# Cross attention: dividing by the softmax's sums in feature layout, after a trip through DRAM

## The reference

```python
q = split_heads(layernorm(x) @ wq + bq)        # 8 x 16 x 512 x 16
k = split_heads(ctx @ wk + bk)                 # 8 x 16 x 64 x 16
v = split_heads(ctx @ wv + bv)
scores = q @ k.T / sqrt(16) (+ mask)           # the mask in the second layer only
attn = softmax(scores, axis=-1)
x = x + (attn @ v).reshape(8, 512, 256) @ wo + bo
```

## Time and profile before

| | |
|---|---|
| time, median of 3 runs | 2571.32 us (2565.01 to 2572.29) |
| the profiled execution's own time | 2568.06 us |
| its span, first to last instruction | 2566.3 us |
| mean granted TensorE clock | 0.962 of full |
| DMA, mean over the span | 58 GB/s |

### The profile page before, as it was taken

How to read it: one execution, slowest core, us unless ns; L and a number is a source line. 1 busy time by engine, 2 the same in 40 slices (tenths; PEclk the granted TensorE clock), 3 DMA queues, 4 the chain that set the end, 5 groups by cost and what they waited for, 6 DMA issues and landing times. The chain is left out here.

```text
span 2566.3 us, 45589 instructions
## 1 busy us (share of the span) xinstructions
PE 2330.6 (91%) x14571; PEld 1519.5 (59%) x14585; DVE 1457.3 (57%) x3885; ACT 1140.1 (44%) x2685; POOL 734.6 (29%) x848
## 2 busy tenths in 40 slices
PE   7999999889996799899999999888886799999998
PEld 5455555545555566533443333445556599999997
DVE  4766676446765443577777767354545733444333
ACT  1666656523331562277777776422221033333332
POOL 3111111044421321333333221153311433333333
PEclk9999999999998999999999999999995899999999
DMA  6222222120000310322222121100009122222221
GB/s 156 88 87 90 87 76 88 31 76 5 5 1 1 105 44 1 93 63 72 66 76 68 58 73 53 40 7 9 9 1 362 57 36 33 36 36 36 36 35 22
DMA packets 135325, 148.85 MB, mean 58 GB/s; under 512 B 25286, under 2 KB 119152, under 8 KB 135024
## 3 DMA queue, kind: packets, MB, share of 16 engines
q1 hardware_dynamic: 119504, 127.23, 16.1%
q0 software_dynamic: 13680, 17.84, 4.3%
q10 hardware_dynamic: 1968, 1.60, 0.4%
HBM read 100.71 MB, written 46.01 MB: 57 GB/s over the span
## 5 line engine op out<-in xcount | busy, mean ns | idle before, releaser
L452 ACT ACTIVATE self_probs<-self_score_ps 128x512 f32<-128x512 f32 (+3 forms) x1024 | 481.0, 516 | 315.0 <-PE self_score_ps L813 162.7
L618 DVE TENSOR_REDUCE self_neg_max<-self_max_ps 128x1 f32<-128x512 f32 x512 | 328.2, 685 | 147.8 <-PE self_max_ps L799 143.3
L799 PE MATMUL self_max_ps<-self_k_stack,self_q_stack 96*128 96x512 bf16 (+3 forms) x1024 | 347.6, 342 | 21.1 <-DVE self_neg_max L615 12.3
L810 PE MATMUL self_score_ps<-self_q_stack,self_k_stack 99*128 99x512 bf16 (+3 forms) x1024 | 342.5, 342 | 1.6 <-ACT self_probs L452 1.6
L2259 ACT ACTIVATE x_stream<-experts_up_ps,experts_bias_now 128x128 f32<-128x128 f32 x568 | 162.4, 369 | 387.7 <-PE experts_up_ps L2480 387.7
L615 DVE CUSTOM_DVE_ANT_0 self_masked<-self_max_ps,self_later 128x128 f32<-128x128 f32 (+3 forms) x512 | 235.4, 488 | 124.1 <-PE self_max_ps L799 112.7
L2480 PEld LDWEIGHTS experts_up_ps<-experts_tileT,x_stream 128*128 128x128 f32 x2272 | 266.7, 193 | 5.3 <-issue 1.8
L2480 PE MATMUL experts_up_ps<-experts_tileT,x_stream 128*128 128x128 f32 x2272 | 267.2, 276 | 1.4 <-DVE x_stream L2396 1.4
L2490 PE MATMUL experts_down_ps<-experts_down,x_stream 128*128 x1136 | 256.8, 379 | 0.0
L824 PE MATMUL self_out_ps<-self_probs,self_values 128*32 128x512 f32 (+3 forms) x2048 | 231.8, 524 | 3.3 <-ACT self_probs L452 1.4
L810 PEld LDWEIGHTS self_score_ps<-self_q_stack,self_k_stack 99*128 99x128 bf16 x1024 | 98.8, 97 | 229.1 <-ACT self_probs L452 171.2
(11 more groups left out here) (293 smaller groups left out, 3962.7 us busy)
## 6 DMA issues: line engine op xcount, KB each, us to landing
self_parts_dram<-self_parts SPq DMA_DIRECT2D x64, 384.0 KB, 2.3
self_q_stack<-self_parts_dram SPq DMA_DIRECT2D x384, 64.0 KB, 2.3
self_k_stack<-self_parts_dram SPq DMA_DIRECT2D x360, 64.0 KB, 2.3
experts_up<-moe_up_dram SPq DMA_DIRECT2D x8, 1024.0 KB, 8.3
experts_down<-moe_down_dram SPq DMA_DIRECT2D x8, 1024.0 KB, 10.6
x_stream<-x_dram SPq DMA_DIRECT2D x8, 512.0 KB, 7.8
expert_rows_dram<-experts_down SPq DMA_DIRECT2D x8, 512.0 KB
out_dram<-x_stream SPq DMA_DIRECT2D x8, 512.0 KB, 8.6
```

What stands on the lines that cost most here:

```text
L452: act.activation(probs[:, i % 8, 0:w], score_ps[:, (16 * n + i) % 3, 0:w], ACT.Exp).then_inc(exp_done, 1)
L618: dve.tensor_reduce(neg_max[:, n % 2, t, h:h + 1], max_ps[:, i % 2, 0:w], AX, ALU.max, negate=True).then_inc(max_read, 1)
L799: last = pe.matmul(max_ps[:, i % 2, 0:w], q_stack[0:ROWS, h, P * t:P * t + P], k_stack[0:ROWS, h, 0:w], start=True, stop=True)
L810: last = pe.matmul(score_ps[:, m % 3, 0:w], k_stack[0:KROWS, head, P * j:P * j + P], q_stack[0:KROWS, head, S - w:S], start=True, stop=not ...
```

## The change

- `ot` and `ob` are gone, with VectorE's reciprocal and multiplication per quarter, the tiles o_norm, oT, r_sums, and ScalarE's `turned_back`.
- Instead SyncE stores each half of o_raw (128 partitions x 2 x 512, 512 KB) to DRAM when `copy_out` has written it, and loads it again as two tiles of 256 KB: `o_now`, the results alone with features on the partitions in the order that the projection needs, and `sums`, each head's sum broadcast to its 16 feature rows. The loads of a batch wait until the projection of the batch before has been made.
- ScalarE inverts the sums, as exp(-ln(sum)), in `inverted`; VectorE's `normalise` multiplies o_now by sums, once for each half. ("e", b, ·) reads o_now.
- TensorE's order: ("e", b - 1, 1) comes before ("M", b + 1, 3) now, and ot and ob fall out.
- VectorE's order: `statistics(b + 3)` comes after `maxima(b + 1, 1)` and the first normalise, both `add`s come before `maxima(b + 1, 3)`, `layer_norm(b + 3)` directly after it, `valued` last.
- GpSimd's order: `inverse_deviation(b + 3)` comes before `add_bias`, and `spread_keys(b + 3)` after the second `shift`.
- SyncE: context and mask are loaded three batches ahead, and the weights of mixture of depths in iteration 1, behind the first stores.

```diff
-        r_sums = sb("r_sums", [P, 2, 2, 8])
-        o_norm = sb("o_norm", [P, TT, D])
-        oT = sb("oT", [P, KD, S])
+        o_now = sb("o_now", [P, 2, S])
+        sums = sb("sums", [P, 2, S])
+        out_scratch = nc.dram_tensor(f"{name}_out_dram", [2, 8, 2, HD, S], F32).ap()
...
             steps = [("S", b, 0)]
-            steps += [("ob", b - 1, 0)] * last + [("M", b + 1, 0)] * more + [("xt", b + 2, 0)] * next2
+            steps += [("M", b + 1, 0)] * more + [("xt", b + 2, 0)] * next2
             steps += [("PV", b - 1, 1)] * last + [("xt", b + 2, 1)] * next2
             steps += [("S", b, 1)]
-            steps += [("ot", b - 1, 2)] * last + [("M", b + 1, 1)] * more + [("sr", b - 2, 0)] * choice
-            steps += [("ot", b - 1, 3)] * last + [("q", b + 2, 0)] * next2
+            steps += [("M", b + 1, 1)] * more + [("sr", b - 2, 0)] * choice
+            steps += [("q", b + 2, 0)] * next2
             steps += [("S", b, 2)]
-            steps += [("q", b + 2, 1)] * next2 + [("M", b + 1, 2)] * more + [("ob", b - 1, 1)] * last + [("PV", b, 0)]
+            steps += [("q", b + 2, 1)] * next2 + [("M", b + 1, 2)] * more + [("PV", b, 0)]
             steps += [("e", b - 1, 0)] * last
             steps += [("S", b, 3)]
-            steps += [("ot", b, 0)] + [("M", b + 1, 3)] * more + [("bk", b - 2, 0)] * choice + [("e", b - 1, 1)] * last
-            steps += [("ch", b - 2, 0)] * choice + [("ot", b, 1)] + [("v", b + 1, 0)] * more
+            steps += [("e", b - 1, 1)] * last + [("M", b + 1, 3)] * more + [("bk", b - 2, 0)] * choice
+            steps += [("ch", b - 2, 0)] * choice + [("v", b + 1, 0)] * more
...
-        closing = [("ob", B - 1, 0), ("PV", B - 1, 1)] + [("sr", B - 2, 0)] * routed + [("ot", B - 1, 2), ("ot", B - 1, 3), ("ob", B - 1, 1)]
+        closing = [("PV", B - 1, 1)] + [("sr", B - 2, 0)] * routed
...
+                def out_store(b, half):
+                    sp.wait_ge(o_copied, 2 * b + half + 1)
+                    wait(sp, out_loaded[half], 32 * b)
+                    sp.dma_start(out_scratch[half].rearrange("(r i) c d t -> (i c d) r t", r=2),
+                                 o_raw[:, 2 * half:2 * half + 2]).then_inc(out_stored[half], 16)
+                def out_load(b, half):
+                    sp.wait_ge(out_stored[half], 16 * b + 16)
+                    wait(sp, e_full, 2 * b)
+                    sp.dma_start(o_now[:, half], out_scratch[half, :, 0]).then_inc(out_loaded[half], 16)
+                    sp.dma_start(sums[:, half], out_scratch[half, :, 1, 0:1].to_broadcast([8, HD, S])).then_inc(out_loaded[half], 16)
+                for b in range(3):
+                    load(b)
+                for b in range(B):
+                    if b >= 1:
+                        out_store(b - 1, 1)
+                        out_load(b - 1, 1)
+                    out_store(b, 0)
+                    out_load(b, 0)
+                    if b + 3 < B:
+                        load(b + 3)
+                    if routed and b == 1:
+                        for dst, src in router.loads():
+                            sp.dma_start(dst, src).then_inc(depths_loaded, 16)
+                out_store(B - 1, 1)
+                out_load(B - 1, 1)
...
+                    if b + 3 < B:
+                        inverse_deviation(b + 3)
                     if b + 2 < B:
                         add_bias(b + 2)
-                    if b + 3 < B:
-                        spread_keys(b + 3)
                     if b + 1 < B:
                         shift(b + 1, 1)
                     if b + 3 < B:
-                        inverse_deviation(b + 3)
+                        spread_keys(b + 3)
...
+                def inverted(b, half):
+                    act.wait_ge(out_loaded[half], 32 * b + 32)
+                    act.activation(sums[:, half], sums[:, half], ACT.Ln).then_inc(sums_logged, 1)
+                    act.wait_ge(sums_logged, 2 * b + half + 1)
+                    act.activation(sums[:, half], sums[:, half], ACT.Exp, scale=-1.0).then_inc(sums_inverted, 1)
...
                     exponentials(b, 0)
                     if b >= 1:
-                        turned_back(b - 1, 0)
+                        inverted(b - 1, 0)
...
                         queries(b + 2, 0)
+                    if b >= 1:
+                        inverted(b - 1, 1)
                     exponentials(b, 2)
                     if next2:
                         queries(b + 2, 1)
-                    if b >= 1:
-                        turned_back(b - 1, 1)
                     copy_out(b, 0)
...
-                turned_back(B - 1, 0)
+                inverted(B - 1, 0)
                 copy_out(B - 1, 1)
...
+                def normalise(b, half):
+                    dve.wait_ge(sums_inverted, 2 * b + half + 1)
+                    dve.tensor_tensor(o_now[:, half], o_now[:, half], sums[:, half], ALU.mult).then_inc(o_done, 1)
...
                     if more:
                         maxima(b + 1, 1)
                     if b >= 1:
-                        normalise(b - 1, 2)
-                        normalise(b - 1, 3)
+                        normalise(b - 1, 0)
+                    if next3:
+                        statistics(b + 3)
                     if choice:
                         compare(b - 2, (0, 1))
                     if more:
                         maxima(b + 1, 2)
+                    if b >= 1:
+                        normalise(b - 1, 1)
                     if choice:
                         compare(b - 2, (2, 3))
                         choose(b - 2)
                     if b >= 1:
                         add(b - 1, 0)
-                    normalise(b, 0)
+                        add(b - 1, 1)
                     if more:
                         maxima(b + 1, 3)
                     if next3:
-                        statistics(b + 3)
-                    if b >= 1:
-                        add(b - 1, 1)
-                    normalise(b, 1)
+                        layer_norm(b + 3)
                     if more:
                         valued(b + 1)
-                    if next3:
-                        layer_norm(b + 3)
```

More of the change, by code:

```diff
@@ L942, in cross_attention @@
         score_full, exp_done = sem("score_full"), sem("exp_done")
-        pv_full, o_copied, ot_full, sums_inverted, o_done = (sem(s) for s in ("pv_full", "o_copied", "ot_full", "sums_inverted", "o_done"))
-        ob_full, ob_copied, e_full, x_biased, x_done = (sem(s) for s in ("ob_full", "ob_copied", "e_full", "x_biased", "x_done"))
+        pv_full, o_copied, sums_logged, sums_inverted, o_done = (
+            sem(s) for s in ("pv_full", "o_copied", "sums_logged", "sums_inverted", "o_done"))
+        out_stored = [sem(f"out_stored{i}") for i in range(2)]
+        out_loaded = [sem(f"out_loaded{i}") for i in range(2)]
+        e_full, x_biased, x_done = (sem(s) for s in ("e_full", "x_biased", "x_done"))
         if masked:
@@ L1010, in _, with load @@
                     sp.dma_start(router_row[:], router.weights).then_inc(router_loaded, 16)
-                for b in range(B):
-                    if routed and b == 2:
-                        for dst, src in router.loads():
-                            sp.dma_start(dst, src).then_inc(depths_loaded, 16)
+                def load(b):
                     wait(sp, v_full, b - 1)
@@ L1195, in _ @@
                     scores_copied(B - 2)
-                turned_back(B - 1, 1)
+                inverted(B - 1, 1)
                 if routed:
@@ L1412, in value_rows @@
                     last.then_inc(v_full, 1)
-                def turn_out(b, i):
-                    half, pair = i // 2, i % 2
-                    pe.wait_ge(o_copied, 2 * b + half + 1)
-                    for t2 in range(2):
-                        for r in range(2):
-                            at, tok = P * (2 * t2 + r), P * (2 * pair + t2)
-                            last = pe.transpose(general[:, bank("ot", b, i), at:at + P], o_raw[:, 2 * half + r, tok:tok + P], c.ident[:])
-                    last.then_inc(ot_full, 1)
-                def turn_back(b, k):
-                    pe.wait_ge(o_done, TT * b + 2 * k + 2)
-                    for t in range(TT):
-                        last = pe.transpose(general[:, bank("ob", b, k), P * t:P * t + P], o_norm[:, t, P * k:P * k + P], c.ident[:])
-                    last.then_inc(ob_full, 1)
                 def output(b, t):
-                    pe.wait_ge(ob_copied, 2 * b + 2)
+                    pe.wait_ge(o_done, 2 * b + 2)
                     for t2 in range(2):
@@ L1433, in output @@
                         for k in range(KD):
-                            last = pe.matmul(general[:, bank("e", b, t), D * t2:D * t2 + D], oT[:, k, tok:tok + P], wo[:, k],
+                            last = pe.matmul(general[:, bank("e", b, t), D * t2:D * t2 + D], o_now[:, k, tok:tok + P], wo[:, k],
                                              start=(k == 0), stop=(k == KD - 1))
```

25 lines of the change are left out of this document (5 added, 20 removed).

## The result

The kernel after the change took 2584.26 us (median of 5 runs, 2583.15 to 2587.9), the kernel before 2570.36 beside it on the same chip (2565.01 to 2572.29): a ratio of 1.0055, interval 1.0041 to 1.0069. That is 14 us or 0.55 % slower, where I had forecast 7 us faster. The time lies in the range and on the side that I had given 0.28. The profiled execution has a span of 2584.7 us against 2566.3, at a mean granted clock of 0.944 against 0.962.

A forecast was written before the change was run, and what follows sets the result against it. The prediction took TensorE as the fullest engine, VectorE not far behind. Masked +8.5 and routed -15.5 us came to -7, so 2564 us against a median of 2571.32; range 2532 to 2590.

The forecast's parts named there:

- the layer norm that comes beside the shift: VectorE's layer norm and GpSimd's shift block each other: 4.8 us more in masked batches, 3.1 in routed ones.
- The sum, masked: Masked cross attention: a middle batch of 33.9 us against 34.10, the whole stage +8.5 us.
- the first drop lies within the second wait: Masked middle batch: of two clock drops behind TensorE's waits only one counts, 1.6 us added once.
- The trip: Store to DRAM and loads back, 6.7 us from copy to sums, bounds 5 and 10; hidden except in the last batch.
- the +13.2: Masked batch 7 and closing, where nothing covers the trips: +3.6 until the last scores, +9.6 after them.
- 1.6 in about six of ten: Routed middle batches: a clock drop of 1.6 us in about six of ten, part of the 31.2 us forecast.
- their trip hidden behind the routing: Routed closing: the last projections come 5.5 us earlier, the DRAM trip being covered by the routing.
- all into waits: Rival: the transposes' time goes into VectorE waits and lower clock, two drops in each batch; 2575 us, chance 0.25.
- if clock drops are more: Sign of being wrong: more drops of TensorE's clock than the prediction counted.
- The free layer norm: Rival: nothing blocks the layer norm in steady state, masked batches six us less, routed two; 2529 us, chance 0.15.
- The trip that stops ScalarE: Rival: from about 9 us a trip, the inversion holds back the third exponentials and scores in 14 batches; 2588 us, chance 0.20.
- ScalarE's idle time ahead of the logarithm ends by a DMA: Sign of being wrong, if seen in middle batches: ScalarE waits there for the trip's loads.

The follow-up runs named there:

- ln_before_adds: The changed kernel with the layer norm of batch b+3 issued on VectorE before the two adds instead of directly behind the fourth maxima: 2541.39 us, ratio 0.9883.
- kept_clock_sized: The changed kernel, order untouched, with dummy products filling TensorE's masked-stage waits (20 before the first xt, 13 or 20 before the first projection): 2563.64 us, ratio 0.9972.
- the fastest kernel: Changed kernel with layer norm and second normalise earlier, masked add_bias last, the last batch's second copy before its first inversion, and sums loaded first: 2504.15 us, ratio 0.9728.
- before_ln_early: The kernel before, transposes kept, with statistics before the third maxima, layer norm before the adds, inverse deviation before add_bias, spread keys last: 2556.21 us, ratio 0.9937.

## Why the prediction was wrong

**What held.** The transposes and both old waits went. The layer norm takes 6.16 us (6.15 forecast), xt waits for 4.75 (4.9), the projection for 3.15 (3.8), sr for 3.0 in routed batches (2.9), e for 1.0 (1.3). Batches 0 and 1 of the routed one gained 5.3 (5.3). A store's load followed 2.8 us behind it, under the 3.5 given. The mechanism, the layer norm that comes beside the shift, was named and priced as it came, and ln_before_adds shows that it was worth the most.

**The step that failed** is in "The sum, masked": "Waits of 4.9 and 3.8 are longer than the 2.45 that dropped the clock, so I add 1.6 once (the first drop lies within the second wait): 33.9". Nothing of the first drop lies within the second wait: it is 3.15 us in the changed kernel and still 3.15 in ln_before_adds, where there is no first one. That wait is set by the trip and by VectorE, whose starting points are TensorE's own late steps, so it moves along with them. And the second drop costs 2.9, since all of the projection falls into it. 3.4 to 4.3 us and not 1.6 in a middle batch, 20.6 us in the kernel by kept_clock_sized (25 by the spans of the two profiles), of which I had counted 8 (1.6 in each of batches 1 to 5). That is 12 to 17 of the 20 us by which the masked stage is beside its forecast; the waits themselves, 7.9 us together and not 8.7, gave some 4 back. The rows that I took the 1.6 from had v behind the wait, a step of 1.13 us, and the transposes; the price of a drop depends on what stands behind the wait.

**The trip** was mis-sized: 8.5 us where I had 6.7. In middle batches the exponentials did wait for it, without holding up TensorE in the changed kernel. In the last batch it counts: 1.7 us ahead of the last scores, 2.3 (loads of 5.6 for 3.3) and 1.6 in the closing, 5.6 together. With the low clock behind the wait of batch 7 (2.9, which are among the 20.6) that is 8.5, about the 8.3 by which batch 7 and the closing are beside the +13.2.

**Routed.** The middle batches 3 to 5 have 98.6 us together against 93.6, and the same term is the larger part of it. Behind the wait ahead of sr, sr takes 1.08 us for 0.62 in each, q 3.62, 3.03 and 3.62 for 1.98, and the transposes 1.81 and 1.50 for 1.04 in two: 6.9 us, where "1.6 in about six of ten" comes to 3. I had also missed that before has 33.58 us in its batch 4, not 31.90. Batch 7 and what follows it up to the masked stage gained 1.4 and not 6.1; the step "their trip hidden behind the routing" was not tested by itself. Batch 6 gained 1.2 more than forecast.

**The rivals.** The case "all into waits" (2575, "Two drops in each batch") was the right mechanism with too small a price, 1 us for each of 11 batches. It was the last of the signs of being wrong, "if clock drops are more". The free layer norm did not happen, and ln_before_adds with 2541 shows what it is worth; its sum was wrong too, since six less for five batches and two less for five is 40, not 35, and gives 2524. The trip that stops ScalarE was near in time (2588) and wrong as a cause: the trip was 8.5 us, short of the 9 from which I had it decide. Its sign did come, ScalarE's idle time ahead of the logarithm ends by a DMA (2.69 us), but TensorE was waiting on VectorE there.

**What stays open.** How long a wait TensorE can have without a drop behind it is not one number here (below). Batch 7 of the masked one still waits 5.44 us for its trip in the fastest kernel, and in its routed batches waits of 1.05 and 2.03 us ahead of sr are left, behind a router product stopped by GpSimd as in the earlier trace rows.

## What to carry to other kernels

Price a new wait on the fullest engine as the wait and the slow work behind it, read off the steps that will stand there, and add it for each wait until a run shows that one hides another. Give it as a range, for a wait of the same length does not always bring the low clock (below). A step that becomes free to move goes where no other engine starts on the same signal: one line moved was worth 43 us, three times what the change had cost. The round trip through DRAM was worth some 14 us at a good order, 16 more when the part that is needed first was loaded first, and it costs its full length at the end of a stage, where nothing covers it.

## What the runs showed of the hardware

- A wait of 3.15 us ahead of the projections was followed by work at the low clock (3.75 us) where a wait of 4.75 us stood earlier in the same batch, and by work at full clock (1.97) in batches 3 and 4 of ln_before_adds, where none did. But in its batch 2, also without an earlier wait of xt, the projection took 3.51 behind 3.16, and in batch 6 of the fastest kernel 3.47 behind 3.23. Behind 2.68 us q took 1.98 in four of five batches of before, and 2.66 to 3.78 in before_ln_early, whose other wait was shorter. In before's routed batch 4 q took 3.17 (672.10) behind waits of 0.82 and 1.05 us, and 1.88 behind the same waits a batch earlier. So neither the wait's length by itself nor its presence tells.
- The product of two SBUF tiles of 128x512 took 0.69 us with GpSimd idle (1879.52), 1.52 us when `add_bias` on GpSimd had run for 1.4 us already, and 2.88 us when both started together (1774.56 and 1774.55). It ended 0.5 us behind GpSimd's instruction both times. Where it started 0.16 us ahead of GpSimd's shift (1810.03 and 1810.19) it took 0.68, and the shift 4.00 instead of 3.62.
- A product of the 128x128 identity in fp32 takes 0.231 us at full clock (34 in 7.86, clock 1.00), 1.8 times a transpose of a tile of that size (eight in 1.04).
- The load that waits for a store of 512 KB was issued 2.8 us behind it, and 4.5 us behind it with two loads of 256 KB just ahead of the store.
